# A gated cross-attention block on one core: probabilities left undivided, value products turned round, output divided by token

## The reference

```
x = x + tanh(g_xattn) * (softmax(q k^T / 4) v @ wo + bo)    q from layernorm(x), k and v from the context
x = x + tanh(g_ffn) * (expert(layernorm(x)) + relu(layernorm(x) @ sw1 + sb1) @ sw2 + sb2)
```

## Time and profile before

| | |
|---|---|
| median of three runs | 400.85 us |
| span of the profiled execution | 400.4 us |
| PE busy | 355.8 us (89%) |
| PEld busy | 313.7 us (78%) |
| DVE busy | 241.8 us (60%) |
| ACT busy | 186.7 us (47%) |
| POOL busy | 162.4 us (41%) |
| mean granted TensorE clock | 0.972 |

### The profile page before, as it was taken

The page is one execution under the profiler, slowest core; times in us unless marked ns, Lnnn a source line. Parts: engine busy times, 40 slices in busy tenths (PEclk is TensorE's granted clock), DMA queues, the critical chain, the costliest instruction groups (busy, mean ns, idle before and its releaser), DMA issues. The chain is left out here.

```text
span 400.4 us, 7423 instructions
## 1 busy us (share of the span) xinstructions
PE 355.8 (89%) x2341; PEld 313.7 (78%) x2341; DVE 241.8 (60%) x592; ACT 186.7 (47%) x398; POOL 162.4 (41%) x164
## 2 busy tenths in 40 slices
PE   3697868799999999999999999963999999999990
PEld 3475756577889878889868988853999999999990
DVE  0789897669758979668784377640244444445440
ACT  3323544265654346635247238610555456546550
POOL 8132365541612412615026042871244455444452
PEclk9989998999999999999999999995899999999997
DMA  6810170059500030000300012723211222221120
GB/s 157 262 25 10 37 237 12 8 148 249 149 9 11 3 108 12 9 4 4 106 2 0 2 54 58 283 94 118 52 50 43 66 79 69 58 64 43 61 63 10
DMA packets 34541, 28.31 MB, mean 71 GB/s; under 512 B 15562, under 2 KB 32073, under 8 KB 34521
## 3 DMA queue, kind: packets, MB, share of 16 engines
q1 hardware_dynamic: 31737, 21.16, 19.3%
q0 software_dynamic: 2784, 6.91, 5.5%
HBM read 16.02 MB, written 9.82 MB: 65 GB/s over the span
## 5 line engine op out<-in xcount | busy, mean ns | idle before, releaser
L1006 DVE TENSOR_TENSOR hT_lo<-h,hT_hi 128x256 fp32r<-128x256 f32 (+1 forms) x104 | 57.5, 555 | 65.5 <-ACT h L686 60.7
L582 POOL TENSOR_TENSOR probs<-probs,rinv 128x616 f32<-128x616 f32 x32 | 40.9, 1282 | 111.9 <-DVE rinv L902 111.9
L683 ACT ACTIVATE hT_hi<-h_ps,vec_cols 128x256 fp32r<-128x256 f32 (+1 forms) x68 | 39.2, 577 | 61.8 <-PE h_ps L1114 55.7
L753 ACT ACTIVATE probs<-probs 128x616 f32<-128x616 f32 x32 | 23.0, 720 | 53.0 <-DVE probs L953 53.0
L1114 PE MATMUL bank<-k_diag,qT 128*128 128x308 f32 x128 | 39.8, 434 | 3.0 <-ACT qT L700 2.2
L1114 PE MATMUL y_ps<-ew_hi,hT_hi 128*128 128x256 f32 x144 | 42.1, 292 | 0.0
L1114 PE MATMUL y_ps<-ew_hi,hT_lo 128*128 128x256 f32 x144 | 40.3, 280 | 0.0
L1114 PE MATMUL y_ps<-ew_lo,hT_hi 128*128 128x256 f32 x144 | 40.2, 280 | 0.0
L1114 PE MATMUL y_ps<-sw_hi,hT_hi 128*128 128x256 f32 x128 | 38.2, 299 | 1.8 <-DVE hT_lo L1006 1.6
L686 ACT ACTIVATE h<-h_ps,vec_cols 128x256 f32<-128x256 f32 (+1 forms) x68 | 39.0, 574 | 0.0
L1114 PE MATMUL bank<-pT,v_diag 128*128 128x256 f32 (+1 forms) x160 | 36.0, 380 | 0.6 <-ACT pT L723 0.5
(11 more groups left out here) (168 smaller groups left out, 958.4 us busy)
## 6 DMA issues: line engine op xcount, KB each, us to landing
stage<-in_L_ffn_w SPq DMA_DIRECT2D x4, 1024.0 KB
sorted_dram<-empty_rows SPq DMA_DIRECT2D x10, 257.0 KB, 4.7
xs<-sorted_dram SPq DMA_DIRECT2D x10, 257.0 KB
stage<-in_L_ffn_sw SPq DMA_DIRECT2D x2, 1024.0 KB
xn_all<-xn SPq DMA_DIRECT2D x4, 512.0 KB, 3.7
part_dram<-x_all SPq DMA_DIRECT2D x4, 512.0 KB, 3.0
x_all<-in_x SPq DMA_DIRECT2D x2, 512.0 KB, 9.1
x_all<-in_x SPq DMA_DIRECT2D x1, 1024.0 KB, 12.8
```

What stands on the lines that cost most here:

```text
L582: nc.gpsimd.tensor_tensor(pq, pq, rinv[:, b, k, :].unsqueeze(2).to_broadcast([P, HG, KEYS]), ALU.mult).then_inc(p_ready, 1)
L683: nc.scalar.activation(hT[0][:, c % HB, 0:width], hidden_bank(c % banks)[:, 0:width], ACT.Relu, bias=b1_sb[:, m, c:c + 1]).then_inc(h_hi, 1)
L753: nc.scalar.activation(probs[:, b, k, :], probs[:, b, k, :], ACT.Exp, scale=HEAD_DIM ** -0.5).then_inc(p_exp, 1)
L1006: nc.vector.tensor_tensor(hT[1][:, c % HB, 0:width], h32[:, c % 2, 0:width], hT[0][:, c % HB, 0:width], ALU.subtract).then_inc(h_lo, 1)
```

## The change

Probabilities stay undivided. Each value gets a 17th column of ones beside its 16 (`VW`), so `v_diag`, now only as wide as the two or three heads of a chunk, yields output and sum together. `pT` is the stationary operand and `v_diag` moves; a tile of tokens lands in a bank of its own (t = 0 in bank 3, t = 1 in bank 2) as tokens x (16 heads x 17). DVE takes the reciprocal of the 16 sums of a token and multiplies (`divide`); a new step `oturn` transposes the result back into bank 3. DVE's sums, their reciprocals and POOL's multiplication go. ACT copies `pT` two chunks at a time. The lists are rearranged. Cut to its core:

```diff
+VW = HEAD_DIM + 1
+SPANS = [(c * P // KEYS, (min(GK, c * P + P) - 1) // KEYS + 1) for c in range(CHUNKS)]
...
-ORDER = [("scores", 0, 1, 0), ("soft", 0, 1, 0), ("exp", 0, 1, 0), ("values", 0, 0, 0), ("norm2", -1, 0, 0),
-         ("scores", 0, 1, 1), ("norm2", -1, 0, 1), ("soft", 0, 1, 1), ("exp", 0, 1, 1), ("norm", 1, 0, 0),
+ORDER = [("scores", 0, 1, 0), ("soft", 0, 1, 0), ("exp", 0, 1, 0), ("norm2", -1, 0, 0), ("norm2", -1, 0, 1),
+         ("scores", 0, 1, 1), ("soft", 0, 1, 1), ("exp", 0, 1, 1), ("values", 0, 0, 0), ("norm", 1, 0, 0),
...
-                    if step == "exp":
-
-                        pool.wait_ge(p_rinv, (2 * j + b) * 4 + k + 1)
-                        pq = by_head(probs[:, b, k, :])
-                        nc.gpsimd.tensor_tensor(pq, pq, rinv[:, b, k, :].unsqueeze(2).to_broadcast([P, HG, KEYS]),
-                                                ALU.mult).then_inc(p_ready, 1)
...
-                        for v in range(2):
-                            r = ROWS[(2 * u + v) % CHUNKS]
-                            nc.scalar.activation(pT[0:r, 2 * u + v, :], bank[2 + u % 2][0:r, v * SEQ:(v + 1) * SEQ],
-                                                 ACT.Copy).then_inc(pT_sb, 1)
-                if step == "values":
-                    act.wait_ge(o_ps, 2 * j + b + 1)
+                        nc.scalar.activation(pT[:, 2 * u:2 * u + 2, :].rearrange("p c s -> p (c s)"),
+                                             bank[2 + u % 2][:, :], ACT.Copy).then_inc(pT_sb, 1)
+                if step == "oturn":
+                    act.wait_ge(oT_ps, 2 * j + b + 1)
...
-            def sums(i, b, k):
-                dve.wait_ge(p_exp, (2 * i + b) * 4 + k + 1)
-                nc.vector.tensor_reduce(out=rsum[:, b, k, :], in_=by_head(probs[:, b, k, :]), axis=AX_X, op=ALU.add
-                                        ).then_inc(p_sum, 1)
-                dve.wait_ge(p_sum, (2 * i + b) * 4 + k + 1)
-                nc.vector.reciprocal(rinv[:, b, k, :], rsum[:, b, k, :]).then_inc(p_rinv, 1)
+            def divide(i, b, t):
+                nth = TB * (2 * i + b) + t + 1
+                dve.wait_ge(o_ps, nth)
+                heads = bank[3 - t][:, 0:HEADS * VW].rearrange("p (h d) -> p h d", d=VW)
+                nc.vector.reciprocal(rinv[:, t, :], heads[:, :, HEAD_DIM:VW].rearrange("p h o -> p (h o)")
+                                     ).then_inc(o_rinv, 1)
+                dve.wait_ge(o_rinv, nth)
+                nc.vector.tensor_tensor(o_sb[:, t, :].rearrange("p (h d) -> p h d", d=HEAD_DIM),
+                                        heads[:, :, 0:HEAD_DIM],
+                                        rinv[:, t, :].unsqueeze(2).to_broadcast([P, HEADS, HEAD_DIM]), ALU.mult
+                                        ).then_inc(o_rdy, 1)
...
                     pe.wait_ge(v_in[b], 16 * len(PIECES) * (j + 1))
-                    pe.wait_ge(pT_sb, 2 * CHUNKS * (2 * j + b + 1))
+                    pe.wait_ge(pT_sb, CHUNKS * (2 * j + b + 1))
+                    if b == 0 and not start:
+
+                        pe.wait_ge(x2T_lo, KC * j)
+                    for t in range(TB):
+                        for g in range(GROUPS):
+                            for c in range(CHUNKS):
+                                h0, h1 = SPANS[c]
+                                ins = mm(bank[3 - t][:, (g * HG + h0) * VW:(g * HG + h1) * VW],
+                                         pT[0:ROWS[c], g * CHUNKS + c, t * P:(t + 1) * P],
+                                         v_diag[0:ROWS[c], b, g, c, 0:(h1 - h0) * VW], (g, c) == (0, 0),
+                                         c == CHUNKS - 1, skip_group_check=True)
+                        ins.then_inc(o_ps, 1)
+                if step == "oturn":
+
+                    pe.wait_ge(o_rdy, TB * (2 * j + b + 1))
                     for g in range(GROUPS):
-                        for c in range(CHUNKS):
-                            ins = mm(bank[3][:, g * SEQ:(g + 1) * SEQ], v_diag[0:ROWS[c], b, g, c, :],
-                                     pT[0:ROWS[c], g * CHUNKS + c, :], c == 0, c == CHUNKS - 1)
-                    ins.then_inc(o_ps, 1)
+                        for t in range(TB):
+                            ins = nc.tensor.transpose(bank[3][:, g * SEQ + t * P:g * SEQ + (t + 1) * P],
+                                                      o_sb[:, t, g * P:(g + 1) * P], ident[:, :])
+                    ins.then_inc(oT_ps, 1)
...
                     pe.wait_ge(xn2_ready, j + 1)
-                    if k == 1 and more_scores:
-
-                        pe.wait_ge(o_lo, 2 * j + 3)
+                    if more_scores:
+
+                        pe.wait_ge(pT_sb, CHUNKS * (2 * j + 3))
```

More of the change, by code:

```diff
@@ L52 @@
 CHUNKS = -(-GK // P)
+VW = HEAD_DIM + 1
+SPANS = [(c * P // KEYS, (min(GK, c * P + P) - 1) // KEYS + 1) for c in range(CHUNKS)]
+SPAN = max(h1 - h0 for h0, h1 in SPANS)
 TURNS = [(0, 1), (2, 3), (4,)]
@@ L88 @@
          ("exp", 0, 0, 2), ("norm", 1, 0, 0), ("scores", 0, 0, 3), ("soft", 0, 0, 3), ("in", 1, 0, 0),
-         ("exp", 0, 0, 3), ("sums", 0, 0, 3), ("scores", 0, 1, 0), ("soft", 0, 1, 0), ("query", 1, 0, 0),
+         ("exp", 0, 0, 3), ("scores", 0, 1, 0), ("soft", 0, 1, 0), ("query", 1, 0, 0),
          ("exp", 0, 1, 0), ("turn", 0, 0, 0), ("scores", 0, 1, 1), ("turn", 0, 0, 1), ("soft", 0, 1, 1),
@@ L92 @@
          ("scores", 0, 1, 2), ("soft", 0, 1, 2), ("exp", 0, 1, 2), ("stats", 0, 0, 2), ("values", 0, 0, 0),
-         ("in", 1, 1, 0), ("scores", 0, 1, 3), ("soft", 0, 1, 3), ("exp", 0, 1, 3), ("cut", 0, 0, 0),
-         ("query", 1, 1, 0), ("sums", 0, 1, 3), ("out", 0, 0, 0), ("scores", 1, 0, 0), ("soft", 1, 0, 0),
+         ("scores", 0, 1, 3), ("oturn", 0, 0, 0), ("soft", 0, 1, 3), ("exp", 0, 1, 3), ("in", 1, 1, 0),
+         ("cut", 0, 0, 0), ("query", 1, 1, 0), ("out", 0, 0, 0), ("scores", 1, 0, 0), ("soft", 1, 0, 0),
@@ L95 @@
          ("exp", 1, 0, 0), ("turn", 0, 1, 0), ("scores", 1, 0, 1), ("soft", 1, 0, 1), ("exp", 1, 0, 1),
          ("turn", 0, 1, 1), ("scores", 1, 0, 2), ("soft", 1, 0, 2), ("exp", 1, 0, 2), ("turn", 0, 1, 2),
-         ("scores", 1, 0, 3), ("soft", 1, 0, 3), ("exp", 1, 0, 3), ("sums", 1, 0, 3), ("stats", 0, 0, 3),
-         ("values", 0, 1, 0), ("out", 0, 1, 0), ("bias", 1, 0, 0), ("bias", 1, 1, 0), ("turn", 1, 0, 0),
+         ("values", 0, 1, 0), ("scores", 1, 0, 3), ("oturn", 0, 1, 0), ("soft", 1, 0, 3), ("exp", 1, 0, 3),
@@ L106 @@
          ("turn", 0, 1, 0), ("exp", 1, 0, 0), ("y", -1, 0, 2), ("turn", 0, 1, 1), ("scores", 1, 0, 1),
          ("soft", 1, 0, 1), ("turn", 0, 1, 2), ("exp", 1, 0, 1), ("h", -1, 0, 5), ("norm", 1, 1, 0),
-         ("values", 0, 1, 0), ("scores", 1, 0, 2), ("soft", 1, 0, 2), ("exp", 1, 0, 2), ("y", -1, 0, 3),
-         ("out", 0, 1, 0), ("h", -1, 0, 6), ("in", 1, 1, 0), ("scores", 1, 0, 3), ("soft", 1, 0, 3),
-         ("y", -1, 0, 4), ("query", 1, 1, 0), ("exp", 1, 0, 3), ("sums", 1, 0, 3), ("h", -1, 0, 7),
+         ("values", 0, 1, 0), ("scores", 1, 0, 2), ("y", -1, 0, 3), ("oturn", 0, 1, 0), ("soft", 1, 0, 2),
@@ L936, in iteration @@
                         aggregate(range(2 * TP, TILES))
-                    if step == "sums":
-                        sums(j, b, k)
+                    if step == "values":
+                        for t in range(TB):
+                            divide(j, b, t)
                     second_half(step, j, b, k, early)
```

77 lines of the change are left out of this document (45 added, 32 removed), and 8 rows, old and new, of the table END.

## The result

Four runs of the changed kernel have a median of **446.77 us** (446.24 to 452.26); beside them the kernel before has 400.67 (400.16 to 403.09). The ratio is **1.1175, 95% interval 1.1129 to 1.1222**: 46 us slower. The forecast, 416.4 us with a range to 426, has the sign and not the size. The profiled execution is the one of 446.24 us; its span is 444.5 us.

What follows compares the result with a forecast made beforehand. TensorE's own time per batch and its new waits ahead of the last gate were taken as the bound. Terms -1.2 + 3.9 + 5.8 + 5.6 + 1.4 = +15.5 us gave 416.4 us, range 404 to 426.

Steps and rivals of the forecast that it cites:

- What bounds the kernel: Whole kernel: TensorE's own time per batch counts, and every new wait of TensorE ahead of the last gate.
- the prediction's own sign: Between 90 and 242 us: TensorE busy 99% there would show the forecast waits at the pass heads to be wrong.
- the walk of the heads: Start of a pass: TensorE idles 0.8 us before the second scores and 2.1 us before the value products.
- Removal, -1.2: POOL's multiplications and DVE's sums go; TensorE gains only its waits for POOL's division, 1.2 us.
- Records, +0.2 a batch: Value products: 40 records at 0.115 us, paced by weight loads, take 4.6 us for 4.39 before.
- Rival (d): Value products: a narrow record costs only its columns, 1.4 us a batch; faster, 390.8 us; chance 0.10.
- the adding up in (a): Value products: load and stream add up, 8.4 us more over six batches, 425 us; chance 0.17 shared with a clock case.
- Turn back, +3.9: Four added transposes a batch, 0.44 us; with the records' 0.2, 0.65 for each of six batches.
- Heads, 2.9 each: Start of the passes beginning at 136 and 190 us: 2.9 us of new TensorE waits each, +5.8.
- Start, +5.6: Before the first pass: out's second result comes at 79.3, the first pass's value products at 90.6; +5.6 us.
- Last norm2, +1.4: Between last out and norm2: one h of 1.37 us moves ahead of out, uncovering DVE's root; +1.4 us.
- rival (a): Slower still: load and stream add up (425 us), or half clock after gaps costs up to 5 us (421.5); chance 0.17.

Runs made afterwards that it cites:

- experiment 13: Kernel before with its sums, reciprocals and POOL's division left out, order and old products kept: 398.67 us (0.9942).
- experiment 6: Kernel before, old order, with its value products as 40 records of 128 moving columns: 402.48 us (1.0025).
- experiment 11: Changed kernel with 128 columns and three reorderings: out ahead of h 6, values ahead of norm2, start's fourth scores ahead of its second values: 416.62 us (1.0372).
- experiment 2: Changed kernel with its new order, but the old wide value products (20 records of 256 columns a batch): 427.14 us (1.0642).
- experiment 10: Changed kernel with 128 columns, out put ahead of h step 6 again in the loop's list: 420.64 us (1.0454).
- experiment 3: Changed kernel with each of the 40 value-product records filled up with zeros to 128 columns: 429.55 us (1.0695).

## Why the prediction was wrong

**What bounds the kernel** held: TensorE's time and its waits ahead of the last gate set the end. Of the 44.1 us of span, 40.6 lie before the last value products. From the first pass to there TensorE is busy 155.3 of 170.6 us, 91%: by the prediction's own sign the walk of the heads is not refuted.

**Removal, -1.2:** measured -2.4 (experiment 13). Right in kind.

**Records, +0.2 a batch:** right; 0.114 us a record at full clock, and 1 us in all in experiment 6. The weight load's pace set it, as the earlier trace rows had it: 34, 64 and 128 columns take 4.55, 4.57 and 4.63 us for 40 records. The Trainium skill ("TensorE: Matmul & The Clock Gate", section "LDWEIGHTS (loading the stationary operand)", 107 ns for 128 columns) is near it, 7 ns under the measured 114. The figure of about 25 ns for up to 64 columns in its section "Back-to-back issue gap" is given there for products without their loads, so I should not have read it as a price for a new block with each record. Rival (d) and the adding up in (a) are out.

**Turn back, +3.9:** four transposes stand 0.36 us ahead of the next instruction at full clock (138.31 to 138.67), 0.44 forecast. No wait for the division in front of it in the changed kernel, as forecast; where experiment 11 puts the start's turn directly behind its products, it is 0.8 us, also as forecast.

**Heads, 2.9 each:** 0.88 + 1.73 = 2.6. Right.

**Start, +5.6:** with wide products (experiment 2) the scores of (1,0) start at 59.97 (forecast not before 59.9), out's second result at 80.54 (79.3), the value products at 91.71 (90.6). The sizes are near, in part by luck. The rows of experiment 2, and the first of them in the kernel before:

```profile
54.80 0.55 PE L1121 MATMUL bank<-xnT_hi,wqo_hi 128*128 128x256 f32 x1 [4.57 <-DVE xnT_lo L869]
...
59.97 1.20 PE L1121 MATMUL bank<-k_diag,qT 128*128 128x308 f32 x4
...
69.45 6.25 PE L1121 MATMUL bank<-pT,v_diag 128*128 128x256 f32 x20 [1.94 <-ACT pT L724]
```

```profile
54.74 0.36 PE L1114 MATMUL bank<-xnT_hi,wqo_hi 128*128 128x256 f32 x1 [1.24 <-DVE xnT_lo L868]
```

The start's list also moves the step in to directly ahead of query, whose products wait for it; the prediction didn't walk this. TensorE idles 4.57 us there, then has a clock of 0.50 from 54.8 to 59.8, and comes to the scores at 59.97 without a wait in front of them. The second products start when forecast (69.45 for 69.55), although TensorE waits 1.94 us for pT in front of them, since the fourth scores no longer stand there; the walk had no such wait. They then take 6.25 us for 4.6, at a mean clock of 0.72, and this half clock more than covers the 1.1 us by which the walk is short. In the changed kernel itself the scores start at 62.34 and the products of the first pass at 97.48; the waits are the same, so I put the difference to 91.71 down to half clock.

**Last norm2, +1.4:** its wait is 1.9 (the longer one in the row of xn) for 0.3 before, +1.6. Right.

**Left out: out behind h in DVE's queue.** I walked that exchange of steps only for the last norm2. In the loop it puts out's result behind hT_lo on DVE, and the step in waits 3.2 us for it in each of two passes: 6.5 us of gap, 8.9 us of time by experiment 10. The prediction doesn't name this place: outside the heads it costed the loop's new order at nothing without a cover for it.

**The step that failed: the clock, "up to 5 us" in rival (a) and nothing in the sum.** I worked out the half clock from one gap with wide products around it and asked only whether gaps would bring it. The narrow records were priced by their time alone, at full clock. Measured, their narrowness is worth 17 us in this order (experiment 3). The gaps under padded or wide products cost, as an estimate, up to 6 to 9 us of clock more (mean clock 0.97 and 0.96 over 295 us: 2 x 0.03 x 295 = 18 us and 24 us at half clock, for 5 before; half of the difference). The sum by the runs: before to 40 records of 128 columns, +1; to the new order with its turn, division and gaps, +27 (429.6 for 402.5), where the forecast's other terms had 14; to 34 and 51 columns, +17. Of the 13 us by which the middle term was too small, 8.9 are out behind h. The rest of some 4 us was not taken apart by a run; the estimate for the clock, which overlaps with the 8.9, would cover it.

The range ended at 426 because I had put the clock and the adding up beside each other as alternatives of one rival, each small. It should have held both together, and room for one wait not walked.

## What to carry to other kernels

A product form with few moving columns per weight load is not priced by its time at full clock: measure the granted clock around it. Here it cost 5 us in two orders with few or shorter gaps (and 16 in one execution of six) and 17 beside gaps of 0.9 to 3.2 us. If such records are paced by their loads anyway, try filling them up with zero columns: here that cost 0.1 us per 40 records and gave 17 back. When a list is reordered, walk each engine's own queue for every exchanged pair, in each pass: a result behind another engine's chain waits for all of it.

## What the runs showed of the hardware

- 40 records of fp32 products (two for each product), each with its own load of a 128x128 block, take 4.55 us at 34 and 51 moving columns, 4.57 to 4.65 at 64 and 4.63 to 4.70 at 128: as the columns hardly count, the load sets the pace.
- The granted clock's half level came back over and over while TensorE was never idle for more than 3.2 us: between 60 and 270 us the changed kernel has a mean clock of 0.88, 2 x 0.12 x 210 = 50 us at half clock, and its repeat 0.85, 63 us. Up to the scatter it is 56 us of 310 with narrow records and gaps (74 in the repeat), 24 with the gaps and wide products (experiment 2), 18 with the gaps and 128 columns (experiment 3), 2 x 0.05 x 265 = 26 with narrow records alone, most of it in the start, 5 with neither.
- Behind the same wait of 1.73 us for x2T_lo, 40 records took 6.77 us with 34 and 51 columns (97.48) and 4.70 with 128 (experiment 3).
- With narrow records and gaps a kernel's time is not steady: 443.56 to 453.52 us for the same kernel, and two edits that took gaps away gave no gain that could be measured.
